# An attention and FFN kernel on one core: in two of each eight steps a ScalarE instruction normalises the fourth head, and two engines' orders are rewritten around it

## What is computed

```
q, k, v = x Wq^T, x Wk^T, x Wv^T          (32 query heads, 8 key/value heads of 128)
q, k    = rope(rmsnorm(q)), rope(rmsnorm(k))
scores  = q [cached k (512 keys, through a page table), new k (128)]^T / sqrt(128), masked
o       = softmax(scores) [cached v, new v];   a = o Wo^T
s       = silu(a w_gate^T) with the half of largest |s| in each row set to 0
x       = x + (s * (a w_up^T)) w_down^T
x       = x + int4_linear(adapter(x))
```

## Time and profile before

| | |
|---|---|
| median of three runs | 1375.73 us (1375.11 to 1376.3) |
| the profiled execution | 1375.81 us, its span 1374.0 us |
| TensorE (PE) busy | 1358.3 us, 99% |
| VectorE (DVE) busy | 1227.5 us, 89% |
| ScalarE (ACT) busy | 870.7 us, 63% |
| GpSimd (POOL) busy | 784.2 us, 57% |
| granted TensorE clock | 1.00 |

### The profile page before, as it was taken

One profiled execution on the slowest core, in us unless ns is written; L12 is line 12 of the kernel. 1 busy time (PEld: TensorE's weight loads), 2 busy tenths in 40 slices (PEclk: granted clock), 3 DMA queues, 4 the chain that ended last, 5 costly groups with the idle time before them and its releaser, 6 DMA issues.

```text
span 1374.0 us, 23448 instructions
## 1 busy us (share of the span) xinstructions
PE 1358.3 (99%) x8015; PEld 1183.2 (86%) x8015; DVE 1227.5 (89%) x2624; ACT 870.7 (63%) x2224; POOL 784.2 (57%) x813
## 2 busy tenths in 40 slices
PE   9899999999999999999999999999999999999998
PEld 6788888888888888888888888888888888888888
DVE  8999898989898989898989898999899987987783
ACT  7777676767676767676767676767777662222221
POOL 7867666666676667666766666667666610111111
PEclk9999999999999999999999999999999999999999
DMA  6111111111111111111111111112121321111212
GB/s 217 47 47 45 55 55 47 47 55 55 47 46 55 55 47 47 54 54 47 47 55 54 47 47 55 55 47 66 54 73 32 114 96 45 47 47 49 76 42 75
DMA packets 34035, 80.46 MB, mean 59 GB/s; under 512 B 10259, under 2 KB 11539, under 8 KB 32499
## 3 DMA queue, kind: packets, MB, share of 16 engines
q1 hardware_dynamic: 17522, 45.29, 10.5%
q0 software_dynamic: 16384, 33.59, 8.2%
HBM read 76.74 MB, written 2.10 MB: 57 GB/s over the span
## 4 chain that ended last, share of the span: by engine, by line
PE 89%; DVE 6%; ACT 2%; issue 1%; DMA 1%; POOL 0%; DVEq 0%; SPq 0%; ACTq 0%
PE proj_ps L111 10%; PE proj_ps L113 10%; PE proj_ps L112 10%; PE turn_ps L770 9%; PE score_ps L113 5%; PE score_ps L112 5%; PE score_ps L111 5%; PE value_ps L111 5%; PE value_ps L112 5%; PE value_ps L113 5%; PE gu_ps L111 3%; PE gu_ps L113 3%; PE gu_ps L112 3%; PE out_ps L1035 2%; PE turn_ps L732 2%; PE turn_ps L739 2%
## 5 line engine op out<-in xcount | busy, mean ns | idle before, releaser
L561 POOL DMA_INDIRECT kg<-kc,idx x256 | 264.5, 1033 | 263.8 <-issue 248.4
L1286 ACT ACTIVATE probs<-probs,shift,rstd 128x640 f32<-128x640 f32 x256 | 234.5, 918 | 132.7 <-DVE shift L1730 132.7
L571 POOL DMA_INDIRECT vg<-vc,idx x256 | 253.4, 990 | 70.7 <-issue 70.7
L1766 DVE TENSOR_TENSOR pt_lo<-turn_ps,pt_hi 128x512 fp32r<-128x512 f32 x320 | 217.7, 686 | 41.5 <-ACT pt_hi L1292 40.0
L1292 ACT ACTIVATE pt_hi<-turn_ps 128x512 fp32r<-128x512 f32 x320 | 186.5, 593 | 86.7 <-PE turn_ps L770 86.4
L1741 DVE CUSTOM_DVE_ANT_0 probs<-score_ps,mask 128x640 f32<-128x640 f32 x256 | 206.6, 821 | 10.5 <-PE score_ps L113 8.6
L770 PE MATMUL turn_ps<-cst,probs 128*128 128x128 f32 x1280 | 191.5, 272 | 1.7 <-DVE probs L1759 1.0
L111 PE MATMUL proj_ps<-w_hi,xt_parts 128*128 128x512 f32 x496 | 188.9, 381 | 0.7 <-ACT qk L1242 0.7
L770 PEld LDWEIGHTS turn_ps<-cst,probs 128*128 128x128 f32 x1280 | 157.2, 141 | 28.2 <-DVE probs L1759 2.2
L113 PE MATMUL proj_ps<-w_hi,xt_parts 128*128 128x512 f32 x496 | 168.1, 339 | 0.0
L112 PE MATMUL proj_ps<-w_lo,xt_parts 128*128 128x512 f32 x496 | 167.1, 337 | 0.0
(11 more groups left out here) (255 smaller groups left out, 3314.7 us busy)
## 6 DMA issues: line engine op xcount, KB each, us to landing
w_raw<-wqkv SPq DMA_DIRECT2D x28, 384.0 KB, 3.3
wo_raw<-wo SPq DMA_DIRECT2D x32, 256.0 KB, 3.1
wa_sb<-wa SPq DMA_DIRECT2D x7, 1024.0 KB, 5.0
kg<-kc,idx POOLq DMA_INDIRECT x256
vg<-vc,idx POOLq DMA_INDIRECT x256
wg_raw<-wg SPq DMA_DIRECT2D x2, 1376.0 KB, 6.3
wu_raw<-wu SPq DMA_DIRECT2D x1, 2752.0 KB, 9.9
wd_raw<-wd SPq DMA_DIRECT2D x1, 2560.0 KB, 12.9
```

The source lines that it names most:

```text
L561: pool.indirect_dma_start(kg[:, b % 2, c, :], None, kc, bass.IndirectOffsetOnAxis(ap=idx[:, s // B % 2, b * NC + c:b * NC + c + 1], axis=0))\
L571: pool.indirect_dma_start(vg[:, b % 2, c, :], None, vc, bass.IndirectOffsetOnAxis(ap=idx[:, s // B % 2, b * NC + c:b * NC + c + 1], axis=0))\
L1286: act.activation(row, row, ACT.Exp, bias=shift[:, h:h + 1], scale=rstd[:, b % 2, h:h + 1], accum_out=sums[:, h:h + 1])\
L1766: dve.tensor_tensor(pt_lo[:, at, :], turn_ps[1 - j % 2][:, :], pt_hi[:, at, :].bitcast(F32), ALU.subtract).then_inc(p_lo_done[j], 1)
```

## The change

ScalarE, in the step with b = 4: the rounding of weight piece 0 moves from behind the rounding of probability chunks 3 and 4 to between the exponentials and chunk 3. In the steps with b = 4 and b = 5 of groups 0 to 6 ScalarE also multiplies the fourth head of the next step's probabilities by its reciprocals (`scale_fourth`, a copy with a pointer for its scale), with b = 4 between chunks 3 and 4, with b = 5 between the exponentials and chunk 3. VectorE leaves that head out there and signals `probs_done` behind the third. TensorE's first transpose of those probabilities waits for a further semaphore, `head_scaled`. VectorE's list for b = 4 is rewritten: `split_w(g + 1, 0)` goes from ahead of the keys' roundings to behind them, `rotate_q` from ahead of `split_o` to behind the first two `maxima` and so next to `split_w(g + 1, 1)`.

```diff
+def fourth_by_act(s):
+    return s // B + 1 < HK and s % B in (B - 3, B - 2)
+
+def fourths(s):
+    return 2 * (s // B) + s % B - (B - 3) + 1
...
                     def turn_probs(s, b, j):
                         if j == 0:
                             wait(pe, probs_done, s + 1)
+                            if fourth_by_act(s):
+                                wait(pe, head_scaled, fourths(s))
...
+                    def scale_fourth(s, b):
+                        wait(act, recip_done, s + 1)
+                        row = probs[:, b % 2, REP - 1, :]
+                        act.activation(row, row, ACT.Copy, scale=recips[:, REP - 1:REP]).then_inc(head_scaled, 1)
...
                         if live(s + 1):
                             exps(s + 1, b1, (2, 3))
+                        if next_w:
+                            split_w(g + 1, 0)
+                        elif fourth_by_act(s + 1):
+                            scale_fourth(s + 1, b1)
...
                             split_probs(s, b, 3)
+                        if next_w:
+                            scale_fourth(s + 1, b1)
...
                             split_probs(s, b, 4)
...
-                        if next_w:
-                            split_w(g + 1, 0)
...
+                        final = REP - 2 if fourth_by_act(s) else REP - 1
...
-                        if h == REP - 1:
+                        if h == final:
                             last.then_inc(probs_done, 1)
...
                     def step_with_first_w(s, b, g):
...
-                        normalise(s + 1, b1, (0, 1, 2))
+                        normalise(s + 1, b1, (0, 1))
                         split_probs(s, b, 3)
-                        normalise(s + 1, b1, (3,))
+                        normalise(s + 1, b1, (2,))
                         split_probs(s, b, 4)
-                        split_w(g + 1, 0)
                         split_cached_k(s + 2)
                         split_q(s + 2)
                         split_new_k(s + 2)
+                        split_w(g + 1, 0)
+                        split_o(s)
+                        maxima(s + 2, b2, (0, 1))
                         rotate_q(s + 3, b3)
-                        split_o(s)
-                        maxima(s + 2, b2, (0,))
                         split_w(g + 1, 1)
-                        maxima(s + 2, b2, (1,))
                         split_probs(s + 1, b1, 0)
...
                     def step_with_last_w(s, b, g):
...
                         split_cached_k(s + 2)
-                        normalise(s + 1, b1, (3,))
                         split_q(s + 2)
```

More of the change, by code:

```diff
@@ L185, in adaln_attn_ffn @@
         probs_done = semaphore("probs_done")
+        head_scaled = semaphore("head_scaled")
         p_turned = [semaphore(f"p_turned{j}") for j in range(NJ)]
```

## The result

The changed kernel takes 1386.03 us (median of four runs, 1385.57 to 1386.79), the kernel before on the same chip 1375.81 (1375.11 to 1376.3): a ratio of 1.0077, 95% interval 1.0066 to 1.0089, 10.2 us slower. The forecast was 1387.4 with a range of 1378.0 to 1391.5. The profiled execution took 1386.79 us, its span 1385.0.

A forecast was written before the change was run, and what follows sets the result against it. TensorE, busy 99% of the span, was taken to bound the kernel. Seven losses of 2.05 us (0.75 serial chain, 1.3 port) make 14.4, less 2.8 gained: 11.6 on 1375.81, 1387.4 us, range 1378 to 1391.5.

The forecast's parts named there:

- What bounds, and the 3.27 us to be had: TensorE, 99% busy, bounds; seven b = 4 intervals exceed 17.13 by 3.27 us in all, of which 2.8 is gained.
- The multiplication's price: ScalarE's copy with a pointer for the fourth head: 0.82 us, or 0.72 to the next start.
- The serial chain: Behind b = 4's second maximum everything comes 0.80 later, chunk 3 also waits for `scale_fourth`; TensorE loses 0.75 us seven times.
- The walk: Count through the new list from the output projection's first product: third maximum at 4.62, cached keys 0.71 late.
- Its three instructions less don't help: At b = 5, VectorE's shorter list before chunk 3's low part gains nothing, since it waits for ScalarE.
- The port: GpSimd's `v_lo` meets the rotation behind the second maximum and holds VectorE up: 1.3 us, seven times, bounds 0 and 1.8.
- My mark for a wrong step: The port step would be wrong if the rotations take 0.68 and the b = 5 interval 17.9.
- The sum: 14.4 lost less 2.8 gained = 11.6 us on 1375.81, giving 1387.4 us, 0.8% slower.
- (a): Rival: GpSimd yields, the rotation is not held up; +2.5 us, 1378.3 us; chance 0.11.
- (b): Rival: faster, chunk 3 at b = 5 is not late for TensorE; only the gain remains, 1373.0 us; chance 0.05.
- (c): Rival: each of seven rotations pays step 24's 1.8 us; +15 us, 1391 us; chance 0.08.
- (d): Rival: VectorE stays behind TensorE, so the new order doesn't bind; time unchanged within 1 us; chance 0.03.

The follow-up runs named there:

- run 1: The changed kernel with VectorE's list for b = 4 back in its old order, ScalarE as changed: 1375.74 us, ratio 0.9992 to the kernel before.
- run 4: As run 1, with ScalarE's multiplication of the fourth head at b = 4 moved behind chunk 4: 1374.01 us, ratio 0.9984.
- run 8: The kernel before with only ScalarE's early weight piece 0 from the change, all heads on VectorE, old list: 1374.23 us, ratio 0.9991.
- run 5: The changed kernel with GpSimd's `v_lo` left out but for one column in the seven steps with b = 4: 1376.91 us, ratio 1.0011.
- run 6: As run 5, and with b = 5 ScalarE's multiplication stands behind the rounding of chunk 3: 1374.34 us, ratio 0.9993.
- Run 2: The changed kernel with `v_lo` held until VectorE has written weight piece 1, in the seven steps with b = 4: 1380.97 us, ratio 1.0031.
- run 7: As run 4, and in step 24 alone `v_lo` waits for the rotation's third product: 1371.77 us, ratio 0.9974.

## Why the prediction was right, point by point

- **What bounds, and the 3.27 us to be had.** Right. The gain was 2.60 against 2.8: groups 0 and 1 keep 0.47 and 0.20, I had left 0.25 in each.
- **The multiplication's price.** 0.82 forecast, 0.82 to 0.83 in all fourteen, 0.72 to 0.74 to the next start. The estimate of 0.81 from the Trainium skill (ScalarE: Activation LUTs) agrees. The Trainium skill's rule (the same page, Rules for kernel authors) that multiplications belong on VectorE holds at b = 5 of the rewritten list, where the place costs 0.39, while with the old list (run 1) the same place costs nothing; at b = 4 it fails: run 4's intervals are 0.12 to 0.37 shorter than run 8's, which differs by the fourth head on VectorE and the order of the multiplications.
- **The serial chain.** The walk said 0.75, runs 5 and 6 show 0.68. It located the third maximum within 0.02 us (4.64 against 4.62) and said rightly that ScalarE's rounding of chunk 3 decides. "Its three instructions less don't help" holds only while the multiplication stands ahead; without it only 0.28 remains, since the two multiplications that stood 1.45 in the kernel before take 1.06 when they come later. The walk took their old length for granted.
- **The port.** 1.3 forecast, 1.25 measured by run 5. The size was right, and so was its working: the rotation begins at 2.02 (404.23 less 402.21) where 2.0 was worked out, and loses 0.26 to the second `v_lo` against 0.3. The place was not: I expected a rotation of 1.7 to 2.0, but `v_lo` began while the second maximum was under way, and the `shift` behind that took the wait, 1.15 instead of 0.15. Run 2 shows that it was `v_lo`. The sign that I had named, rotations of 1.7 to 2.0, did not come. My mark for a wrong step asked for two things, rotations of 0.68 and an interval of 17.9; the first came true, and only the second, the interval's length of 19.05, kept a right step from being dropped.
- **The sum.** 7 x 1.92 - 2.6 = 10.8 against 7 x 2.05 - 2.8 = 11.6; the median came 1.4 us under the forecast, of which the sum explains 0.7 to 0.8.
- **The rivals.** (a) would have shown 17.8: that is run 5, what the change would have been had GpSimd not met it. (b) asked for a chain 0.7 shorter and a `v_lo` that misses the rotation; run 6, with no `v_lo` and no multiplication ahead of chunk 3, still has 0.28 each. (c) and (d) are excluded by the intervals.

## What to carry to other kernels

Before an instruction is moved between two that another engine waits for, count what then stands in a row from the one to the other, and look on GpSimd's timeline for what runs at the same time on the same memory; here 1.27 us of harmless work became 1.92 us of stop in each of seven steps. A mark that is to prove a mechanism is better set on the sum of a stretch than on one instruction: here the wait fell on the `shift` ahead of the rotation that it was expected on. And once a collision is understood, look for it in the kernel before: one added wait at one step took 0.9 us off its interval (run 7), nearly what ScalarE's early piece gave in all seven (run 8, 1.2).

## What the runs showed that I had not expected

The wait between VectorE and GpSimd fell on a one-column instruction: `shift` took 1.15 us beside a `v_lo` that was under way, 0.15 with `v_lo` elsewhere. It could have been read in the trace of the kernel before. The prediction says of the old list that only a `shift` met `v_lo`; it did not look at how long that took. In an ordinary step:

```profile
382.25 0.61 DVE L1730 SCALAR_TENSOR_TENSOR shift<-row_max,rstd 128x1 f32<-128x1 f32 x1
```

```profile
381.51 1.32 POOL L579 TENSOR_TENSOR v_lo<-vg,v_hi 128x512 fp32r<-128x512 f32 x1
```

Fifty `shift`s of that trace begin inside a `v_lo`. All of them end within 0.04 us of its end and take 0.29 to 1.31 us. The ordinary intervals stay at 17.13 all the same.

The reading of a head's scores, which was in flight when `v_lo` began, wasn't prolonged (0.82), nor was `v_lo` (1.29); behind a weight piece in flight `v_lo` takes 1.77 instead. The Trainium skill (GPSIMD Engine Reference, specifications) speaks of contention for instructions with two SBUF inputs. The scores are read from PSUM with a mask from SBUF, which fits it. `shift` reads a column each of `row_max` and `rstd`, so its size gives no protection.

Who waits is not settled. The `shift` behind a running `v_lo`, and `v_lo` behind a running weight piece, look as if whichever is under way goes first. Step 24 does not fit that: the rotation's row begins 0.36 us ahead of `v_lo`'s, and yet the rotation was the long one. GpSimd was at an indirect DMA's issue when it began:

```profile
468.35 0.94 POOL L561 DMA_INDIRECT kg<-kc,idx  x1 [0.30 <-issue]
```

Perhaps the rotation was already waiting for that issue and `v_lo` went ahead of it; no run tested this.
